# VectorE adds the turned shift ahead of a burst's two maxima instead of between them

## What is computed

```python
# layer 1, per image and head (head_dim 16, N = 256)
attn = softmax(einsum('bhnd,bhdm->bhnm', q, k) * scale)
out = einsum('bhnm,bhmd->bhnd', attn, v)
out = einsum('bchw,oc->bohw', out, W_proj) + b_proj

# layer 3, the same with a window of 32 keys
sw_mask = (j <= i) & (j > i - WIN)
logits = where(sw_mask, einsum('bthc,bshc->bhts', q, k) / sqrt(C), -inf)
out = einsum('bhts,bshc->bthc', softmax(logits), v) @ W_o
```

## Time and profile before

| | us |
|---|---|
| median of three runs | 635.94 |
| lowest and highest run | 634.18 and 640.32 |
| the profiled execution, its own time | 634.05 |
| its span, first to last instruction | 632.3 |

### The profile page before, as it was taken

The page is one execution under the profiler, slowest core; times in us unless marked ns, Lnnn a source line. Parts: engine busy times, 40 slices in busy tenths (PEclk is TensorE's granted clock), DMA queues, the critical chain, the costliest instruction groups (busy, mean ns, idle before and its releaser), DMA issues. The chain is left out here.

```text
span 632.3 us, 10008 instructions
## 1 busy us (share of the span) xinstructions
PE 570.3 (90%) x3288; PEld 314.2 (50%) x3288; DVE 422.5 (67%) x902; ACT 337.8 (53%) x585; POOL 280.5 (44%) x624
## 2 busy tenths in 40 slices
PE   7987998888586999999999999999799889869997
PEld 6754455554466444444444444444345566634433
DVE  2654557774365776776999799979745875564643
ACT  3542455666243786666756685668414555543221
POOL 4466003232132577778686878687421342420000
PEclk9998999999697899999999999999899999979999
DMA  6900000000000000000000000000000000000000
GB/s 164 276 3 0 1 1 2 3 1 1 2 2 1 0 1 0 0 1 2 0 1 0 1 2 1 0 1 1 0 1 2 3 2 2 3 0 2 17 18 33
DMA packets 10246, 8.63 MB, mean 14 GB/s; under 512 B 4042, under 2 KB 8148, under 8 KB 10196
## 3 DMA queue, kind: packets, MB, share of 16 engines
q1 hardware_dynamic: 10196, 8.00, 4.5%
HBM read 6.94 MB, written 1.05 MB: 13 GB/s over the span
## 5 line engine op out<-in xcount | busy, mean ns | idle before, releaser
L1584 POOL TENSOR_TENSOR h_s<-g_s 128x512 f32<-128x512 f32 x128 | 163.8, 1283 | 58.0 <-ACT g_s L1502 38.3
L1502 ACT ACTIVATE g_s<-z_s,b 128x1024 f32<-128x1024 f32 x128 | 146.5, 1149 | 63.6 <-DVE z_s L1419 38.5
L1419 DVE TENSOR_TENSOR z_s<-bank,PB 128x1024 f32<-128x1024 f32 x128 | 153.4, 1217 | 30.0 <-PE bank L1333 29.6
L1333 PE MATMUL bank<-XN_C,W 128*128 128x512 f32 x256 | 132.7, 605 | 0.3 <-PEq L1110 0.3
L1342 PE MATMUL bank<-h_s,W 128*128 128x512 f32 x256 | 130.3, 593 | 0.1
L1001 DVE TENSOR_REDUCE shiftpad<-bank 128x2 f32<-128x512 f32 (+1 forms) x128 | 72.2, 587 | 59.1 <-PE bank L815 30.4
L977 ACT ACTIVATE ET_all<-bank 128x512 f32<-128x512 f32 (+1 forms) x128 | 59.2, 514 | 74.1 <-PE bank L832 43.0
L1342 PEld LDWEIGHTS bank<-h_s,W 128*128 128x128 f32 x256 | 48.5, 190 | 62.0 <-issue 56.0
L1333 PEld LDWEIGHTS bank<-XN_C,W 128*128 128x128 f32 x256 | 47.7, 194 | 51.8 <-issue 44.4
L1057 POOL TENSOR_SCALAR var<-mv 128x2 f32<-128x2 f32 x14 | 3.3, 234 | 104.0 <-DVE mv L1041 104.0
L827 PE MATMUL bank<-Qp,Kp 17*128 17x256 f32 x256 | 36.2, 400 | 7.2 <-DVE Qp L1014 7.2
(11 more groups left out here) (331 smaller groups left out, 974.4 us busy)
## 6 DMA issues: line engine op xcount, KB each, us to landing
W<-in_L_ffn_W_dram SPq DMA_DIRECT2D x1, 2048.0 KB, 9.0
out_dram<-QK SPq DMA_DIRECT2D x4, 256.0 KB, 2.1
XN_T<-in_x_dram SPq DMA_DIRECT2D x3, 256.0 KB, 5.0
XN_T<-in_x_dram SPq DMA_DIRECT2D x2, 128.0 KB, 2.1
Wgate<-in_L_ffn_W_gate_dram SPq DMA_DIRECT2D x1, 256.0 KB, 4.4
Wup<-in_L_ffn_W_up_dram SPq DMA_DIRECT2D x1, 256.0 KB, 5.2
Wdown<-in_L_ffn_W_down_dram SPq DMA_DIRECT2D x1, 256.0 KB, 3.8
wraw<-in_L_conv_W_qkv_dram SPq DMA_DIRECT2D x1, 192.0 KB
```

Of the source, the lines that this page charges most:

```text
L1333: nc.tensor.matmul(bank[s % 4][:, :], W1[:, f // 4, f % 4 * P:(f % 4 + 1) * P], XN_C[:, g * W:(g + 1) * W], start=True, stop=True).then_in ...
L1419: nc.vector.tensor_tensor(z_s[:, s % RING, :].rearrange("p (w n) -> p w n", w=2), bank[s % 4][:, None, :].broadcast_to([P, 2, W]), PB[:, g ...
L1502: nc.scalar.activation(g_s[:, s % RING_G, :], z_s[:, s % RING, :], ACT.Gelu, bias=b1[:, f:f + 1]).then_inc(s_g, 1)
L1584: nc.gpsimd.tensor_tensor(h_s[:, s % RING, :], g_s[:, s % RING_G, 0:W], g_s[:, s % RING_G, W:2 * W], ALU.add).then_inc(s_h, 1)
```

## The change

In each burst VectorE waits for the turn and adds it to `Qp` before it takes the first of the burst's two maxima. Before, it took the first maximum, then added, then took the second. No instruction is added, dropped or altered, and the other engines' streams are as they were. Burst 32, which has an addition and no maxima, is as before.

```diff
@@ -1005,14 +1005,13 @@
                     for s in range(LAST):
                         if late is not None and s >= 1:
                             late.dve(dve, s - 1)
-                        if s < BURSTS:
-                            highest(2 * s)
                         if (g := half_at(s, AT_MT)) is not None:
                             image, half = g // 2, g % 2
                             q = Qp[:, half, image * N:(image + 1) * N]
                             dve.wait_ge(s_MT, g + 1)
                             nc.vector.tensor_tensor(q, bank[7][:, 0:N], q, ALU.add).then_inc(s_sh, 1)
                         if s < BURSTS:
+                            highest(2 * s)
                             highest(2 * s + 1)
                         if s == WARM:
                             dve.wait_ge(s_warm, len(drive))
```

## The result

| | before | changed |
|---|---|---|
| median of the first comparison, us | 635.87 | 650.27 |
| its six executions, us | 633.96 to 640.44 | 641.39, 645.56, 645.56, 654.98, 683.17, 683.25 |
| the profiled execution, us | 634.05 | 645.56 |
| its span, us | 632.3 | 643.8 |

The ratio of the comparison is 1.0123, 95% interval [1.0074, 1.0171]. The forecast was 639.5 with a range up to 643.5, so it was wrong: the kernel is slower, as forecast, but by two and a half times as much in the profiled execution (+11.5 instead of +4.7) and up to ten times in others (+49).

The account below looks back on a forecast made before the run. TensorE paces the attentions, and VectorE's addition paces it once every two bursts. Layer 1's +4.72 and layer 3's -0.1 or zero gave +4.7: 638.8 on 634.05, 640.6 on the median; 639.5 taken between, range 635 to 643.5.

Parts of the forecast that it names:

- The gain of 0.30: Layer 1: VectorE's addition would start at 113.54 instead of 113.84, 0.30 us sooner in the 12 turns that aren't early.
- The new wait of u1: +0.29: Layer 1: score matmul u1 waits for its bank's maximum, now behind the addition; seven bursts each end 0.29 us later.
- The normalised output: +0.16: Layer 1 after bursts 16, 20, 24, 28: VectorE delivers the output later, so values start 0.16 us later, 0.64 in all.
- Layer 1, +4.72: Sum of layer 1's attention: 2.03 + 1.14 + 0.64 + 0.31 + 0.60 = +4.72 us from held scores and late outputs.
- Layer 3, -0.1: Layer 3's attention: earlier additions gain 1.41 us, held scores cost 1.32, leaving -0.1 or zero.
- The price of 1.32: Layer 3: u1 waits 0.12 us for the maximum in each of 11 turns without the transpose, 1.32 us.
- The clock: 0: TensorE's clock over the attentions: no term in the sum, a little of a fall held in the upper bound.
- Rival 4: TensorE's clock falls under the new pattern of gaps; no size given, chance 0.04 shared with the rest.
- The rule on weight loads: TensorE may pull u1's weight load ahead past its wait, taking about 0.10 us off 9 layer-1 bursts.
- The weights ready (1): u1's weights load before its release, 0.10 us less in 9 layer-1 bursts: +3.8, 637.9 us; chance 0.10.
- the other side (2): The held score costs nothing in either attention, so only gain and output waits remain: -2.0, 632.1 us; chance 0.14.
- the broken overlap (3): Held u1 breaks up side-by-side score matmuls: 3.9 us more in layer 1, up to 2.6 in layer 3, about 645; chance 0.12.

Follow-up runs that it names:

- the four banks: Changed kernel with layer 1's scores going round four banks instead of three from burst 10 on: median 638.00 us, ratio 1.0027.
- Version for gain: Against the kernel before: addition first in layer 3 and, from layer 1's burst 10, with four banks and reordered second maxima; median 635.72 us, ratio 0.9969.
- Half of the turns: Against the kernel before: addition first only in layer 1's bursts 2, 6, 10, ..., 30; 640.23 to 663.96 us, median 659.44.

## Why the prediction was wrong, point by point

- **What bounds the kernel.** Right. TensorE sets the pace in both attentions, and its wait for the addition is the one that the change acts on.
- **The gain of 0.30.** Right as a start time: the wait behind the turn fell from 0.81 to 0.52. As time won it was nearly nothing in the bursts after turns 10, 14, ..., 30, since v1 waited for ScalarE; this was missed. It cost the forecast nothing, as u1 came later still; that was luck, and it spoiled the forecast of the four banks.
- **The new wait of u1: +0.29.** Right, to the hundredth (2.61 less 2.32).
- **The normalised output: +0.16.** Right: an image grew by 0.44 against 0.45.
- **Layer 1, +4.72.** Right at full clock. With the clock held (three dummies in all of bursts 2 to 30) the turn of burst 30 comes 77.21 us after that of burst 2, against 72.91 before: +4.30, where the forecast's terms up to burst 28 are 4.72 - 0.29 = 4.43. From first to last scores it is +4.1, since the bursts ahead of the first turn took 0.5 less in that execution.
- **Layer 3, -0.1.** Wrong by 0.9. The gain of 1.41 was there: over the 15 turns the additions start 1.41 sooner behind their turns, and the scores behind them 1.24. Between first and last scores 1.0 is left of it; where the rest went these runs don't show. The price of 1.32 was not there. After the turn of burst 18 the mask of u1 does load later, 0.40 behind v0's instead of 0.28, but the scores behind it start no later. The changed kernel, then the kernel before:

```profile
523.03 0.11 PEld L841 LDWEIGHTS bank<-bandTb,identb 128*128 128x128 bf16 x2 [0.82 <-DVE QK L1012]
...
523.19 0.10 PEld L847 LDWEIGHTS bank<-bandb,identb 128*128 128x128 bf16 x1
...
523.43 0.10 PEld L847 LDWEIGHTS bank<-bandb,identb 128*128 128x128 bf16 x1
...
523.68 0.19 PEld L829 LDWEIGHTS bank<-QK 17*128 17x128 f32 x2 [0.15 <-issue]
```

```profile
512.41 0.19 PEld L829 LDWEIGHTS bank<-QK 17*128 17x128 f32 x2 [0.26 <-issue]
```

  From the first mask load to the first score load pass 0.65 us, as before (511.76 to 512.41). The 0.12 went into idle time of weight loading, 0.26 before and 0.15 now. The step charged a delay in full without looking at the slack behind it.
- **The clock: 0.** This is the step that failed. The sum put nothing for it, and the upper bound "a little". Rival 4, the lower clock, was dismissed with "I see no reason for it", and its chance of 0.04 shared with the rest. The argument was that gaps of 0.81 us had left the clock at 1.00 and that the new gaps would be shorter. They are shorter, and the clock fell all the same; with the waits left and only dummy work put into them it stood. The profiled execution lost 8.1 us by it; the slowest ones, at a mean clock of 0.88, some 45 by estimate (683.2 against 638.6 with the clock held). With that term at zero the range ended at 643.5, below 11 of the 12 plain executions of the changed kernel.
- **The rule on weight loads** (the Trainium skill, "TensorE: Matmul & The Clock Gate", Part 3, The mechanism). No row shows a load that is pulled ahead past a wait: u1's load and matmul start together, at 106.15, behind its wait, as the full 0.29 says.
- **The rivals.** The weights ready (1) and the other side (2) are refuted by the 0.60 between v0 and u1 and the full 0.29, the broken overlap (3) by the 0.44 by which an image grew. The slow clock, which shared a chance of 0.04 with the rest, is what came.

## What to carry to other kernels

When a change moves a wait inside matmuls that run side by side, price the matmul that is held last in the group, and look for the next wait behind each of them: here the end of VectorE's addition, that of the maximum three units back and that of ScalarE's exponential stood within about 0.6 us of each other. Where the array has many short waits, a forecast of time needs a term for its clock, with a range to one side, even if the trace of before shows 1.00 and the new gaps are shorter. If several executions of before already differ by about a percent with their mean clock, that is the warning. And a wait that can't be removed may be worth filling: 0.4 us of dummy matmuls per image took 14 us off the median of the changed kernel (654.31 to 640.38 in one job), though in the kernel before dummies gained nothing that could be told.

## What the runs showed of the hardware

- A change of 0.45 us in 10.17 of a repeated pattern took TensorE's clock from 1.00 to 0.50, at places and for times that differ between executions: over 118 to 138 us in one profile, over 157 to 187 in another, and with one dummy over 115 to 150.
- Neither the wholly idle gap nor the length of an image puts the kernels in order. Before: gap 0.81, image 10.17, slowest of 23 executions in a job 643.54. Version for gain: gap 0.52, image 9.85, two of 12 at 647. Half of the turns: gap 0.52, image 10.46, five of six at 645 to 664. What in the pattern makes the clock fall stays open. With three dummies in the gap the profiled clock stood at 1.00 in every burst that had them in the changed kernel (95 to 165 us in one run, 65 to 150 in another); with one it fell, and in the kernel before, with three dummies in bursts 2 and 6, it was 0.68 over 75 to 80 us.
- The mean granted clock sorts the executions of one kernel: most of the 29 of before in the last job lie in groups at 633.8 to 634.3 (0.967), 635.8 to 636.0 (0.962), 636.6 to 638.7 (0.957), 640.3 to 640.4 (0.952) and 643.5 to 643.7 (0.946).
